# Scattering the last image's rows in the routing stage of a two-layer attention and expert kernel

## The reference

```
t = t + L2_attn(_ln_t(t));  t = t + L2_ffn(_ln_t(t))      # softmax attention, then 8 experts, one for each token
t = t + L3_attn(_ln_t(t));  t = t + L3_ffn(_ln_t(t))      # dilated attention, then 16 experts, two for each token

# L2_ffn
logits = xt @ Ws + bs;  probs = softmax(logits);  routes = argmax(probs)
y = vmap(lambda w1, b1, w2, b2: gelu(xt @ w1 + b1) @ w2 + b2)(W1, b1, W2, b2)
out = einsum('te,etd->td', one_hot(routes), y) * max(probs)[:, None]

# L3_ffn
top_vals, top_idx = top_k(x @ gate_weight.T, 2);  routing_w = softmax(top_vals)
h_mean = mean over the tokens of an expert of silu(x @ w1[e])
out = einsum('tk,tkd->td', routing_w, (h_mean @ w2)[top_idx])
```

## Time and profile before

| | us |
|---|---|
| Median of 3 runs | 3500.41 (3497.96 to 3501.32) |
| Profiled execution, its own time | 3499.89 |
| Its span | 3498.1 |
| PE busy | 2841.1 (81%) |
| DVE busy | 2207.3 (63%) |
| ACT busy | 1550.4 (44%) |
| POOL busy | 1025.6 (29%) |

### The profile page before, as it was taken

One profiled execution on the slowest core, in us unless ns is written; L12 is line 12 of the kernel. 1 busy time (PEld: TensorE's weight loads), 2 busy tenths in 40 slices (PEclk: granted clock), 3 DMA queues, 4 the chain that ended last, 5 costly groups with the idle time before them and its releaser, 6 DMA issues. The chain is left out here.

```text
span 3498.1 us, 64431 instructions
## 1 busy us (share of the span) xinstructions
PE 2841.1 (81%) x20886; PEld 1554.3 (44%) x20887; DVE 2207.3 (63%) x4232; ACT 1550.4 (44%) x3274; POOL 1025.6 (29%) x1344
## 2 busy tenths in 40 slices
PE   6777869999999999999299767488888888629998
PEld 3334513433344333443199645355555555403336
DVE  6774567787777777774222245577777777527762
ACT  1112526666666666657155322344445444304440
POOL 0001311122222222222233366325566555610000
PEclk9998969999999999999699889888889898759995
DMA  2002462232322323220222123333233232031123
GB/s 78 0 0 85 174 126 40 37 56 39 53 47 40 55 39 53 47 40 8 83 61 61 54 94 105 106 60 62 58 64 60 59 63 56 24 99 52 51 67 109
DMA packets 209250, 215.73 MB, mean 62 GB/s; under 512 B 33456, under 2 KB 185200, under 8 KB 209008
## 3 DMA queue, kind: packets, MB, share of 16 engines
q1 hardware_dynamic: 183376, 176.63, 22.2%
q0 software_dynamic: 14336, 25.72, 2.8%
q10 hardware_dynamic: 11312, 10.35, 1.0%
HBM read 129.26 MB, written 81.90 MB: 60 GB/s over the span
## 5 line engine op out<-in xcount | busy, mean ns | idle before, releaser
L1536 ACT ACTIVATE attn_exps<-attn_sbank 128x392 f32<-128x392 f32 x1600 | 704.7, 503 | 465.4 <-PE attn_sbank L1453 460.7
L1581 DVE TENSOR_REDUCE attn_mx<-attn_rot 128x1 f32<-128x784 f32 x768 | 722.0, 967 | 188.3 <-PE attn_rot L1466 185.5
L1453 PE MATMUL attn_sbank<-attn_q,attn_k 99*128 99x392 bf16 x1536 | 450.1, 333 | 10.7 <-ACT attn_exps L1536 9.5
L1466 PE MATMUL attn_rot<-attn_k,attn_q 96*128 96x392 bf16 x1536 | 401.8, 344 | 69.5 <-DVE attn_mx L1581 39.2
L2282 ACT ACTIVATE dil_exps<-dil_sbank 128x512 f32<-128x512 f32 x512 | 289.3, 597 | 364.6 <-PE dil_sbank L2180 361.1
L2338 DVE TENSOR_REDUCE dil_mx<-dil_rot 128x4 f32<-128x1024 f32 x256 | 307.3, 1218 | 74.2 <-PE dil_rot L2190 72.2
L1493 PE MATMUL attn_acc<-attn_exps,attn_v 128*32 128x392 f32 x3584 | 350.8, 503 | 0.0
L1453 PEld LDWEIGHTS attn_sbank<-attn_q,attn_k 99*128 99x128 bf16 x1536 | 148.8, 98 | 269.8 <-ACT attn_exps L1536 134.5
L2654 PE MATMUL silu_ph<-silu_route_w,silu_xT 128*128 x424 | 238.0, 645 | 21.3 <-issue 12.6
L2190 PE MATMUL dil_rot<-dil_k,dil_q 96*128 96x256 bf16 x1024 | 174.9, 300 | 81.6 <-DVE dil_mx L2338 50.4
L1466 PEld LDWEIGHTS attn_rot<-attn_k,attn_q 96*128 96x128 bf16 x1536 | 117.4, 98 | 276.2 <-DVE attn_mx L1581 179.0
(11 more groups left out here) (367 smaller groups left out, 4804.3 us busy)
## 6 DMA issues: line engine op xcount, KB each, us to landing
attn_q<-q_pieces SPq DMA_DIRECT2D x192, 98.0 KB, 3.5
attn_k<-k_pieces SPq DMA_DIRECT2D x192, 98.0 KB, 4.9
silu_x<-silu_rows SPq DMA_DIRECT2D x212, 64.0 KB, 1.8
dil_q<-dil_q_pieces SPq DMA_DIRECT2D x192, 66.0 KB
dil_k<-dil_k_pieces SPq DMA_DIRECT2D x192, 66.0 KB
q_pieces<-qkv_piece SPq DMA_DIRECT2D x16, 588.0 KB, 3.1
k_pieces<-qkv_piece SPq DMA_DIRECT2D x16, 588.0 KB, 3.2
v_rows<-qkv_v SPq DMA_DIRECT2D x16, 476.0 KB, 3.8
```

The source lines that it names most:

```text
L1453: ins = nc.tensor.matmul(into[:, 0:HS], k_[t.side][g][:, j, c * P:(c + 1) * P], q[t.side][g][:, j, cols], start=True, stop=True)
L1466: ins = nc.tensor.matmul(rot[b][:, hf, 0:HS], q[nxt.side][g][0:QROWS, j, c * P:(c + 1) * P], k_[nxt.side][g][0:QROWS, j, cols], start=True ...
L1536: nc.scalar.activation(e_[:, n % NP, :], sbank[(n + t.side) % 3][:, 0:HS], ACT.Exp, scale=A_DIM ** -0.5).then_inc(s_ex, 1)
L1581: nc.vector.tensor_reduce(into, rot[b][:, :, 0:HS], AX.XY, ALU.max).then_inc(s_free, 1)
```

## The change

The last image's scatters leave both attentions and become the work of POOL in the routing stage. For that, the tiles that they read (`xt`, `posi`), the tile `hold` and three semaphores move out of the attention's memory to a new class, `Scattered`, that is set up before the attention and lives on behind it. POOL no longer waits for landings at the attention's end; SP does so at the end of the routing stage. There ACT waits for the four constants before it issues the weights, and the spare tiles are zeroed by one transfer that reads the same zero rows 8 or 16 times. The addition into `hold` now reads the tile `place`.

```diff
+class Scattered:
+    def __init__(self, m, ex):
+        two = range(2)
+        self.hold = m.sb("hold", [P, 1])
+        self.xt = [m.sb(f"xt{j}", [TOK, NCH, P]) for j in two]
+        self.posi = [m.sb(f"posi{j}", [TOK, ex.picks, NCH], i32) for j in two]
+        self.s_hold = m.sem("held")
+        self.s_sct = [m.sem(f"rows_scattered{j}") for j in two]
...
     def pool_scatter(self, pool, im, n):
-        k, c = divmod(n, NCH)
         if n == 0:
             pool.wait_ge(self.s_xt, im.e + 1)
             pool.wait_ge(self.s_pos, im.e + 1)
+        self.scatter(pool, im, n)
+
+    def scatter(self, pool, im, n):
+        k, c = divmod(n, NCH)
+        if n == 0:
             pool.wait_ge(self.s_hold, im.e + 1)
-            self.nc.gpsimd.tensor_tensor(self.hold[:], self.center[:, 0:1], self.center[:, 0:1], ALU.add).then_inc(self.s_hold, 1)
+            self.nc.gpsimd.tensor_tensor(self.hold[:], self.place[0][:, 0:1], self.place[0][:, 0:1], ALU.add).then_inc(self.s_hold, 1)
         pool.indirect_dma_start(self.xs, bass.IndirectOffsetOnAxis(ap=self.posi[im.side][:, k, c:c + 1], axis=0),
                                 self.xt[im.side][:, c, :], None).then_inc(self.s_sct[im.side], 16)
-    def pool_done(self, pool):
+    def pool_last(self, pool):
+        for n in range(self.SCATTERS):
+            self.scatter(pool, Turn(B - 1), n)
+
+    def scattered(self, eng):
         for j in range(2):
-            pool.wait_ge(self.s_sct[j], self.SCT * PAIRS)
+            eng.wait_ge(self.s_sct[j], self.SCT * PAIRS)
...
@@ route_tail
                 sp.wait_ge(s_set, 1)
-                for n in range(ex.spare):
-                    at = E * REGION + n * TILE
-                    sp.dma_start(xs[at:at + TILE, :], zrow[:]).then_inc(s_zero, 16)
+                spare = xs[E * REGION:E * REGION + ex.spare * TILE, :].rearrange("(n k) d -> k n d", k=TILE)
+                sp.dma_start(spare, zrow[:, :].rearrange("k (o d) -> k o d", o=1).broadcast_to([TILE, ex.spare, P])).then_inc(s_zero, 16)
...
-                sp.wait_ge(s_zero, 16 * (ex.spare + E))
+                sp.wait_ge(s_zero, 16 * (1 + E))
+                router.scattered(sp)
+
+            @block.gpsimd
+            def _(pool):
+                router.pool_last(pool)
 
             @block.scalar
             def _(act):
+                act.wait_ge(s_w, 16 * 4)
                 for dst, src in early:
                     act.dma_start(dst, src).then_inc(s_early, 16)
...
@@ attention
-                if not exps and k == NMX - 1:
-                    out += [("scatter", n, 1) for n in range(NCH)]
...
                 pipe.run(pool, do)
-                router.pool_done(pool)
...
@@ dilated_attention
             if older and not exps and h == D_HEADS - 1:
                 for n in range(D_HEADS):
-                    out += route_steps(n, 1)
+                    out += [x for x in route_steps(n, 1) if x[0] != "scatter"]
...
                 pipe.run(pool, do)
-                router.pool_done(pool)
```

More of the change, by code:

```diff
@@ L727, with __init__ @@
 NEWTON = 3
+class Scattered:
[6 more added lines that the diff above has]
+        self.s_sct = [m.sem(f"rows_scattered{j}") for j in two]
 class Router:
-    def __init__(self, nc, m, a, R, ex, weight, bias, xs, keep, ident=None):
+    def __init__(self, nc, m, outer, a, R, ex, weight, bias, xs, keep, ident=None):
         self.nc, self.a, self.R, self.ex, self.xs = nc, a, R, ex, xs
@@ L749, in __init__ @@
             self.ident = ident
-        self.hold = m.sb("r_hold", [P, 1])
+        self.hold = outer.hold
         self.xc = m.sb("r_xc", [TOK, NCH, P])
-        self.xt = [m.sb(f"r_xt{j}", [TOK, NCH, P]) for j in two]
+        self.xt, self.posi = outer.xt, outer.posi
         self.raw = m.sb("r_raw", [TOK, NCH, E])
@@ L782, in __init__ @@
         self.posf = m.sb("r_posf", [TOK, K, NCH])
-        self.posi = [m.sb(f"r_posi{j}", [TOK, K, NCH], i32) for j in two]
         self.s_w = m.sem("r_weights")
@@ L798, in __init__ @@
         self.s_gate = m.sem("r_gates_ready")
-        self.s_hold = m.sem("r_held")
+        self.s_hold, self.s_sct = outer.s_hold, outer.s_sct
         self.s_ch = m.sem("r_picks_chain")
         self.s_cs = m.sem("r_places_chain")
-        self.s_sct = [m.sem(f"r_rows_scattered{j}") for j in two]
         self.SCT = 16 * NCH * K
@@ L1208, in _, with attention @@
                 ch.done()
-def attention(nc, a, R, qd, kd, vd, xs, keep):
+def attention(nc, outer, a, R, qd, kd, vd, xs, keep):
     HEADS4 = 4
@@ L1339, in attention @@
         LOADS = 16 * 2 * len(Q_SLOTS)
-        router = Router(nc, m, a, R, GELU, "L2_router", "L2_router_b", xs, keep)
+        router = Router(nc, m, outer, a, R, GELU, "L2_router", "L2_router_b", xs, keep)
         WEIGHTS = 16 * 7
@@ L1911, with dilated_attention @@
 D_KR = QROWS + MROWS
-def dilated_attention(nc, a, R, qd, kd, vd, xs, keep):
+def dilated_attention(nc, outer, a, R, qd, kd, vd, xs, keep):
     NP = 16
@@ L2046, in dilated_attention @@
         LOADS = 16 * 2 * len(Q_SLOTS)
-        router = Router(nc, m, a, R, SILU, "L3_router", None, xs, keep, ident32)
+        router = Router(nc, m, outer, a, R, SILU, "L3_router", None, xs, keep, ident32)
         WEIGHTS = 16 * 9
@@ L2777, in softmax_and_routed @@
         keep = dict(place=[m.sb(f"place{j}", [P, GELU.n]) for j in range(2)], region=None, posa=m.sb("posa", [TOK, B, NCH]), gates=gates)
-        attention(nc, a, R, qd, kd, vd, xs, keep)
+        router = attention(nc, Scattered(m, GELU), a, R, qd, kd, vd, xs, keep)
         table = m.sb("table", [1, 2, GELU.tiles], i32)
@@ L2785, in softmax_and_routed @@
         early += [(w2[:, e, :, :], a["L2_w2"][e].rearrange("(c f) d -> f c d", c=4)) for e in range(GELU.n)]
-        route_tail(nc, a, GELU, xs, table, keep, "r1", early, s_early, positions=positions)
+        route_tail(nc, a, GELU, router, xs, table, keep, "r1", early, s_early, positions=positions)
         experts_gelu(nc, a, xs, ys, table, w1b, w2, s_early)
@@ L2796, in dilated_and_routed @@
         keep = dict(place=[m.sb(f"place{j}", [P, SILU.n]) for j in range(2)], region=None, gates_t=gates_d)
-        dilated_attention(nc, a, R, *pieces, xs, keep)
+        router = dilated_attention(nc, Scattered(m, SILU), a, R, *pieces, xs, keep)
         table = m.sb("table", [1, 2, SILU.tiles], i32)
@@ L2805, in dilated_and_routed @@
         early = [(w1[:, e, :], a["L3_w1"][e]) for e in range(SILU.n)]
-        route_tail(nc, a, SILU, xs, table, keep, "r2", early, s_early, counts=counts)
+        route_tail(nc, a, SILU, router, xs, table, keep, "r2", early, s_early, counts=counts)
         experts_silu(nc, a, xs, table, counts, ymean, w1, s_early, gates_d, gates_t, s_gates)
```

4 lines of the change are left out of this document (3 added, 1 removed).

## The result

| | before | after |
|---|---|---|
| Median, us | 3500.86 (3497.96 to 3503.95, 4 runs) | 3455.47 (3450.14 to 3459.27, 4 runs) |
| Profiled execution, its own time | 3499.89 | 3457.31 |
| Its span | 3498.1 | 3455.1 |

The ratio is 0.9872 with an interval of 0.9855 to 0.9889: 45 us, between 39 and 51. The forecast was 3465, with a range of 3457 to 3478.

A forecast was written before the change was run, and what follows sets the result against it. It took POOL's last scatters and the drain after them to bound both attention-to-routing handovers. Gains of 10.0, 20.5, 0.9 and 3.6 sum to 35.0 us, from the median 3465.4, said as 3465, range 3457 to 3478.

The forecast's parts named there:

- the price of POOL's drain: Ends of both routing stages: a new drain there costs 9.2 us (first) or 8.6 us (second), whatever the scatter count.
- a landing: Wait for scatters to land ahead of POOL's drain: 0.8 us taken, between bounds of 0 and 1.6.
- First attention's end: First attention's handover to routing: POOL drops the hold, seven scatters and the wait for landings, gaining 10.0 us.
- Second attention's end: Second attention's handover to routing: POOL drops the hold, fourteen scatters and waits, gaining 20.5 us.
- First routing stage: First layer, first load to experts' first product: the weights' landing sets it, gain 0.9 us, bounds 1.5 and -2.0.
- Second routing stage: Second layer's routing: POOL's path at +28.2 sets its length, against SP's +25.2 and +31.78 before; gain 3.6 us.
- A drain after few scatters costs nothing: Rival on the routing stages: free drains leave the second to SP at +25.2, 3 us better; 3462, chance 0.13.
- Scatters are slow beside the weights: Rival on the routing stages: each scatter issued beside the loads costs 0.84 us more; 3478, chance 0.12.
- The constants land no sooner: Rival on the routing stages: constants stay late, weights start 3.7 us later still; 3468, chance 0.05.
- The moved tiles: Rival on both attentions: tiles at other places run slower, 3510 us if by 2.2%; chance 0.03.
- What would show it: Expected trace signs: four drains of 8 to 10.7 us, routing stages of 20 and 28 us, first product near +24.6.
- three signs of being wrong: Routing-stage scatter spacing over 1.25 us, weights landing after +24, or an attention whose own instructions take longer.

The follow-up runs named there:

- the move alone: Changed kernel with the spare rows zeroed in a loop and without ACT's wait for the constants, against the kernel before: 3469.92 us, ratio 0.9912.
- the other two edits alone: Kernel before with one transfer for the spare rows and ACT's wait for the constants, scatters left in the attention stages: 3489.17 us, ratio 0.9967.
- the best version: Changed kernel without POOL's drains at block ends, 5 of 16 second-layer fills issued by ACT ahead of its weights: 3433.02 us, ratio 0.9825 to the kernel before.

## Why the prediction was wrong, step by step

The direction and the order of the terms were right, but the gain came out 10 us larger than the sum. 3.8 of these are in its terms: 3.4 from one assumption, the price of POOL's drain, 0.8 from a landing, less 0.35. With all four places right the forecast would have been 3461 to 3462, inside the range; the remaining 6 us are in no place that the change touches, and their cause stays open (below).

*The failed step* is "I take 9.2, as in rows 4, since the three rows of drains (112, 224 and 112 such DMAs) do not grow with the count", and with it "It is a price paid once by a block with such DMAs". The rows did not refute a growth with the count: two of them had the same count, and the third is of another layer, whose long drains are all lower. The runs show 0.08 to 0.09 us for each software DMA since the last drain (0.62 for 7, 1.19 for 14, 8.09, 8.65, 9.20 for 98, 105, 112); in the second layer the same step of 0.08 from a lower start (5.80, 6.93, 8.05 for 196, 210, 224); and in any case a drain that lasts until the last one has landed. The two new drains, for which 0.8 of landing and 9.2 or 8.6 were summed, end 4.8 us behind the last scatter, a time set by its landing beside the weights and not by the count. What this changed in each term:

*First attention's end*, 10.0 forecast and 11.4 measured. 0.55 of the excess are the seven scatters that the drain has no longer behind it (9.20 to 8.65), and the landing is wholly beside the drain: 1.6 gained, the upper bound, where I took 0.8.

*Second attention's end*, 20.5 and 21.3. The prediction had POOL's drain end 0.7 us behind SP's store. But the drain is shorter by 1.1 and the landing is beside it, so SP is last, and the gain goes as far as SP lets it: its DRAIN starts at 3058.4 and POOL's ends at 3057.3.

*First routing stage*, 0.9 and 0.55. Right in its mechanism: the wait of POOL for the weights ends last, 15.0 us long in the profile's row. VectorE started at +4.3 (+3.7 forecast), the last weights landed at +23.2 (+22.2), the copy came at +24.1 (+23.9), the product at +24.9 (+24.6). POOL's own path, forecast at +19.2 before the barrier, ended at +14.0; nobody waited for it. (The term's lower bound, -2.0, does not come out of its own rows: 9.2, 1.6, 10.66, 0.9, 4.17 and 0.3 make +26.8, a loss of 1.4.)

*Second routing stage*, 3.6 and 5.6. "So the stage becomes POOL's" is wrong: POOL's drain ends at 3081.97, +22.7, not +27.3. SP's wait ends last, at +25.4, and the stage at +26.2, 1.0 behind the +25.2 that I had for SP's path. The 6.6 us that the prediction gave to the spare rows' single transfer alone were measured with ACT's wait beside it, in the kernel before, and 5.6 of them are kept. I had used the larger drain to cover half of them.

*The rest*, 45 by the median against 38.8 in places. The places' sum lies at the edge of the interval of 39 to 51 us. The traces of before and after show no difference outside the handovers, single ones vary by 14 us, and the comparison of a kernel with itself was off by 0.14%. So chance can make it, but that it does isn't shown; two comparisons of the changed kernel both came out above the places (0.9872 and 0.9865), and what would make other stages faster stays open.

*The rivals.* "A drain after few scatters costs nothing" was the right one in substance: 0.62 and 1.19 us once they have landed, and SP takes over the second stage. Its time, 3462, was also the nearest, and is what the places alone would give. It had 0.13, because I held a row against it (the 10.66 us of the gathering block) which is the price of 112 gathers, paid late. The Trainium skill, VectorE: DVE Perf Modes, "The DRAIN you can't avoid", has "~12 ns constant" for the DRAINs of a program's preamble and postamble. The drains here stand at the ends of the kernel's own blocks, so that sentence did not speak for them, and the trace has other lengths on POOL: 34 ns without software DMAs, 621 behind seven scatters and 9200 behind 112. "Scatters are slow beside the weights" is out for the issue: 0.94 us each, 1.24 apart. Only their landing is slow: 4.2 and 3.7 us from the last scatter's end to its last packet, 1.0 at the attentions' ends. "The constants land no sooner" is out: +4.3 and +5.5 against +7.4 and +7.9. "The moved tiles" are out: the first attention took 1233.6, 1230.3 and 1232.2 us in the three traces of before, 1236.7 and 1237.0 after, and 1230 to 1239 in the other kernels with moved tiles (1233.8 with the move alone), but 1240.6 in the kernel with the other two edits alone, which has the tiles at the old places.

*What would show it.* I said four DRAINs of 8 to 10.7 us. There are four long ones, of 10.5 to 15.8, and I had not thought that a queue that runs ahead makes a DRAIN's row longer than its price. The second stage of 28 us ended by POOL was the sign that was plainly missed. None of the three signs of being wrong appeared (scatters 1.24 to 1.25 us apart, weights landed at +23.2, attentions as long as before): they did not ask which engine ends the second stage.

## What to carry to other kernels

Read a DRAIN on GpSimd from its end back to its engine's last instruction. If software DMAs stand ahead of it, ask how many since the last drain, and whether the last one has landed, not only whether there are any. Shorten the count where it ends a stage, or leave the drain out where semaphores already cover the transfers. Before putting more drains in, look at what queues behind them: ahead of gathers they lost more here than they gave.

When two paths of a stage end within 3 us of each other, a forecast should carry both with their own chances; the cheaper drain turned 3.6 us into 5.6. And a comparison with itself tells how much of a small remainder is worth explaining.

## What the runs showed of the hardware

A drain behind up to 112 software DMAs, all landed, cost 0.08 to 0.09 us for each of them. The second layer's long ones are lower than that alone gives: 8.05 us behind 224, where 0.08 each would be 17.9 (5.80 behind 196, 6.93 behind 210), though the slope from 196 to 224 is the same 0.08. Some 124 of them seem to be paid for elsewhere; where, no run here shows.

Drains repeat to a few ns between kernels: 9200 in three traces of the kernel before, and 10651 to 10657 in the gathering block of all eleven traces that have a single drain there.

The drain's work has no other customer here: without it the next scatters took the same 0.94 us.

In the best version the second experts' stage took 265.0 us from its first product to its last sum, where thirteen other traces have 269.4 to 271.9. The granted clock is 1.00 from 50 us into the stage on, in its trace as in the changed kernel's. Its cause was not looked for; these 5 us are part of the 3429.7 that its trace spans.
